# A fused attention and butterfly-FFN kernel: another order for the beginning of its weight fold

## What is computed

```python
x = x + layernorm(x) * scan(0.9, ctx * ctx)          # scan over the 512 tokens of a sequence
h = layernorm(x) @ W_exp + b_exp                     # 512 -> 2048
h = butterfly(h, up_weights)                         # 11 stages of 2x2 pairs, stride 1, 2, ... 1024
h = gelu(h + up_bias)
h = butterfly(h, down_weights)                       # 11 stages again
x = x + h @ W_con + b_con + down_bias                # 2048 -> 512
```

## Time and profile before

| | us |
|---|---|
| median of 3 executions | 2791.27 |
| lowest, highest | 2789.72, 2792.17 |
| span of the profiled execution | 2791.6 |
| TensorE busy in that span | 2739.0 (98%) |
| VectorE busy | 2129.0 (76%) |
| ScalarE busy | 1134.3 (41%) |
| GpSimd busy | 409.5 (15%) |

### The profile page before, as it was taken

One profiled execution on the slowest core, in us unless ns is written; L12 is line 12 of the kernel. 1 busy time (PEld: TensorE's weight loads), 2 busy tenths in 40 slices (PEclk: granted clock), 3 DMA queues, 4 the chain that ended last, 5 costly groups with the idle time before them and its releaser, 6 DMA issues.

```text
span 2791.6 us, 34984 instructions
## 1 busy us (share of the span) xinstructions
PE 2739.0 (98%) x12141; PEld 2255.2 (81%) x12141; DVE 2129.0 (76%) x3562; ACT 1134.3 (41%) x1697; POOL 409.5 (15%) x578
## 2 busy tenths in 40 slices
PE   8779999999999999999999999999999999999998
PEld 5658888888888888888888888888888888888887
DVE  8958777787877778787777878777887877788533
ACT  4843433434343343434334343433434343343432
POOL 5731111020111102011110201111010111102000
PEclk8989999999999999999999999999999999999999
DMA  9795675847557584765758576575847657585543
GB/s 273 250 299 176 175 223 160 239 152 220 185 173 225 160 241 151 219 188 172 225 162 240 152 216 190 169 226 161 241 152 217 190 167 228 156 244 156 181 151 99
DMA packets 294997, 544.67 MB, mean 195 GB/s; under 512 B 37462, under 2 KB 101110, under 8 KB 277670
## 3 DMA queue, kind: packets, MB, share of 16 engines
q1 hardware_dynamic: 287920, 538.91, 63.5%
q0 software_dynamic: 1488, 2.27, 0.4%
q10 hardware_dynamic: 5414, 1.25, 0.3%
HBM read 447.92 MB, written 60.82 MB: 182 GB/s over the span
## 4 chain that ended last, share of the span: by engine, by line
PE 93%; DVE 1%; DMA 1%; issue 0%; ACT 0%; SPq 0%; POOL 0%; DVEq 0%; ACTq 0%
PE ps L1650 43%; PE ps L1668 25%; PE ps L1681 25%; DMA kv<-in_ctx_dram 1%; DMA w_split<-xop 0%; PE ps L1730 0%; DVE w1r L1121 0%; DVE xop L1121 0%; DVE x L1178 0%; POOL raw L479 0%; SPq L537 0%; DVE raw L1175 0%; DMA raw<-kv 0%; DVE kv L1205 0%; DVE raw L1225 0%
## 5 line engine op out<-in xcount | busy, mean ns | idle before, releaser
L1650 PE MATMUL ps<-xop,w1r 128*128 128x512 f32 x5376 | 1366.8, 390 | 7.1 <-ACT st L946 4.6
L1650 PEld LDWEIGHTS ps<-xop,w1r 128*128 128x128 f32 x5376 | 1011.3, 188 | 218.5 <-issue 6.3
L1681 PE MATMUL ps<-w2r,ghi 128*128 128x512 f32 x2032 | 626.6, 390 | 8.2 <-DVE x L1317 8.2
L1668 PE MATMUL ps<-w2r,ghi 128*128 128x512 f32 x2048 | 630.4, 389 | 0.0
L946 ACT ACTIVATE st<-ps 128x512 f32<-128x512 f32 x384 | 229.8, 598 | 839.0 <-PE ps L1650 839.0
L1317 DVE TENSOR_TENSOR x<-ps,x 128x512 f32<-128x512 f32 x508 | 348.9, 687 | 281.1 <-PE ps L1681 278.6
L1681 PEld LDWEIGHTS ps<-w2r,ghi 128*128 128x128 f32 x2032 | 381.8, 188 | 87.8 <-DVE x L1317 8.6
L1668 PEld LDWEIGHTS ps<-w2r,ghi 128*128 128x128 f32 x2048 | 384.4, 188 | 79.8
L1335 DVE TENSOR_TENSOR g<-ps,st 128x512 f32<-128x512 f32 x384 | 262.9, 685 | 217.3 <-PE ps L1650 217.3
L950 ACT ACTIVATE g<-g,gelu_bias 128x512 f32<-128x512 f32 x384 | 275.1, 716 | 369.4 <-DVE g L1335 369.4
L1340 DVE TENSOR_TENSOR glo<-g,ghi 128x512 fp32r<-128x512 f32 x510 | 345.5, 698 | 79.3 <-ACT ghi L964 79.2
(11 more groups left out here) (160 smaller groups left out, 1619.3 us busy)
## 6 DMA issues: line engine op xcount, KB each, us to landing
w1r<-w_products SPq DMA_DIRECT2D x889, 256.0 KB, 3.3
w2r<-w_split SPq DMA_DIRECT2D x128, 1024.0 KB, 5.0
x<-in_x_dram SPq DMA_DIRECT2D x128, 256.0 KB, 7.1
raw<-kv SPq DMA_DIRECT2D x496, 64.0 KB, 2.2
out_dram<-x SPq DMA_DIRECT2D x120, 256.0 KB, 4.0
kv<-in_ctx_dram SPq DMA_DIRECT2D x64, 256.0 KB, 7.4
raw<-in_ctx_dram SPq DMA_DIRECT2D x64, 256.0 KB, 5.2
w_split<-w2s SPq DMA_DIRECT2D x12, 512.0 KB, 7.3
```

What stands on the lines that cost most here:

```text
L1650: last = nc.tensor.matmul(bank[:, :], w1r[:, slot, w, c * P:(c + 1) * P], xop[:, XPOS[m], v, c, :], start=(opens and i == 0), stop=(i == l ...
L1668: last = nc.tensor.matmul(ps_ya[j][:, :], g[:, p % 2, q, j * P:(j + 1) * P], w2r[:, p % 2, kk, w, :], start=(p == 0 and kk == 0 and i == 0 ...
L1681: last = nc.tensor.matmul(ps_yb[:, :], g[:, p % 2, q, j * P:(j + 1) * P], w2r[:, p % 2, kk, w, :], start=(kk == 0 and i == 0), stop=(kk == ...
```

## The change

Seven pieces, all in the order of the lists; no arithmetic is added or taken away.

1. The up side's top stage is spread bank by bank. Bank places become 4, 0, 1, 2 (`TOP_PLACE[0]`); each waits only until the low product that last read its bank is done (`TOP_FREED`), counts `top_spread` for itself, and `top_products` waits per bank. The pieces stand between the last WT steps: two banks ahead of WT 12, one ahead of WT 14, one behind WT 15.
2. VectorE does `top_products(0)` directly behind `low_products(0)`, and `lane_rows(1)` and both `coefs_lo(1)` after it.
3. ScalarE's `square(0, 0)` moves from ahead of WT 12's copy to behind low_up 1's.
4. VectorE does `high_products(0)` ahead of the first `stats1` (it was behind it). GpSimd's list is unchanged: `rstd_rows(0)`, which waits for that `stats1`, stands ahead of `high_matrix(0)`.
5. The down side's `PARTED` spreads leave their place ahead of the high fold and stand inside it, behind high_up 3. `spread_count` and `SPREAD_ORDER` renumber the waits, so the load of `W_con` waits for all twenty spreads.
6. The down side's top spreads (now four counts) move from behind high_up 9 to behind high_up 15; the bias transpose goes one step later, and the 16 bias matmuls come ahead of high_up 15 where they stood behind it.
7. ScalarE's `square(0, 1)` and `neg_ident` move from behind high_up 3's copy to behind high_up 9's.

```diff
@@ -342,6 +342,11 @@
 
         def spreads(dn, stage):
             return dn * (LOWS + HIGH) + stage + 1
+
+        SPREAD_ORDER = (list(range(LOWS + HIGH)), [*range(PARTED[0]), *range(LOWS, LOWS + HIGH), *PARTED])
+
+        def spread_count(dn, stage):
+            return dn * (LOWS + HIGH) + SPREAD_ORDER[dn].index(stage) + 1
         UP_DONE = LOWS + HIGH
         ALL_DONE = 2 * UP_DONE
 
@@ -358,7 +363,9 @@
             return top_src[dn][0:4].rearrange("q (x b) -> q b x", b=2)
 
 
-        TOP_PLACE = (0, 1, 2, 3)
+        TOP_PLACE = ((4, 0, 1, 2), (0, 1, 2, 3))
+        TOPS = len(TOP_PLACE[0])
+        TOP_FREED = (None, PARTED[0] - 1, PARTED[0], LOWS - 1)
 
 
         def w1_columns(w, r):
@@ -513,7 +520,7 @@
             load_tokens(raw[:, 1, :, :], 0, ctx_rows, 1, ctx_loaded[1])
 
             wcon_src = w_con.rearrange("(k e r) d -> (k e) (r d)", e=E, r=R)
-            sp.wait_ge(coef_spread, spreads(1, LOWS - 1))
+            sp.wait_ge(coef_spread, spread_count(1, LOWS - 1))
             for part in range(2):
                 cols = slice(part * R * D // 2, (part + 1) * R * D // 2)
                 sp.dma_start(flat(wcon[:, :, :])[:, cols], wcon_src[:, cols]).then_inc(wcon_loaded[part], NX)
@@ -834,7 +841,7 @@
                     act.wait_ge(bias_low, 1)
                     wait_kept(act, "high_up", R - 1)
                 if n == 1:
-                    act.wait_ge(top_spread, 2)
+                    act.wait_ge(top_spread, 2 * TOPS)
                 for g in groups:
                     if g == 2:
                         act.wait_ge(wsum_ready, 4 * n + 4)
@@ -873,21 +880,21 @@
                     act.dma_start(bias_tmp, down_bias.partition_broadcast(P)).then_inc(bias_loaded, NX)
                     for stage in PARTED:
                         coefs_hi(1, stage)
-                if k == 3 * KH // 4:
-                    square(0, 0)
                 fold_step("WT", k)
             for k in range(KH):
                 fold_step("low_up", k)
+                if k == 1:
+                    square(0, 0)
             top_hi(1)
             act.dma_start(hc_up, up_w[LOW:LOW + HIGH].rearrange("s (m p) a b -> p s m (a b)", p=P))\
                .then_inc(coef_loaded, NX)
             for r in range(R):
                 fold_step("high_up", r)
-                if r == 3:
+                if r == 9:
                     square(0, 1)
                     act.wait_ge(coef_spread, ALL_DONE)
                     act.activation(neg_ident[:, :], ident[:, :], ACT.Copy, scale=-1.0).then_inc(neg_ident_ready, 1)
-                if r == 12:
+                if r == 13:
                     act.wait_ge(bcol_turned, 1)
                     act.activation(bcol, ps[4][:, 256:256 + 2 * KH], ACT.Copy).then_inc(bcol_kept, 1)
             weights_hi(0, (0, 1))
@@ -1046,7 +1053,7 @@
                     cur = (full if (stages - 1 - stage) % 2 == 0 else spare)[:, 0:n]
                     bank, col = places[stage]
 
-                    dve.wait_ge(coef_spread, spreads(dn, first + max(stage, 3)))
+                    dve.wait_ge(coef_spread, spread_count(dn, first + max(stage, PARTED[0] - 1)))
                     if prev is None:
                         last = nc.vector.tensor_copy(cur.rearrange("p (o a l) -> p o a l", o=outer, a=2),
                                                      spread_view(ps[bank][:, col:col + n], first, stage, outer))
@@ -1091,8 +1098,8 @@
 
             def top_products(dn):
                 dve.wait_ge(path_product, spreads(dn, LOWS - 1))
-                dve.wait_ge(top_spread, dn + 1)
-                for c, bank in enumerate(TOP_PLACE):
+                for c, bank in enumerate(TOP_PLACE[dn]):
+                    dve.wait_ge(top_spread, dn * TOPS + c + 1)
                     last = path_stage(nc.vector, flat(LX[:, dn, 4 * c:4 * c + 4, :]), half[:, 2 * c * P:2 * (c + 1) * P],
                                       spread_view(ps[bank][:, :], 0, LOW - 1, KH // 4), LOW - 1)
                 last.then_inc(low_matrix_ready, 1)
@@ -1238,16 +1245,15 @@
                 nc.vector.tensor_copy(top_sel[lane:lane + Q], top_choice[0:Q]).then_inc(top_sel_ready, 1)
             top_lo(0)
             low_products(0)
+            top_products(0)
             lane_rows(1)
-            coefs_lo(1, PARTED[0:1])
-            top_products(0)
-            coefs_lo(1, PARTED[1:2])
+            coefs_lo(1)
             dve.wait_ge(const_ready, 2)
             dve.wait_ge(bias_row_ready, 1)
             for j in range(J):
                 scan_chunk(0, 0, j)
+            high_products(0)
             stats1(0, 0, xs[0], range(J))
-            high_products(0)
             dve.wait_ge(mean1_ready, J)
             stats1(0, 1, xs[0], range(J), means=False)
             for j in range(J):
@@ -1492,16 +1498,19 @@
                                                     start=(bit == 0), stop=(bit == 1))
                     last.then_inc(coef_spread, 1)
 
-                def top():
+                def top(cs):
                     pe.wait_ge(top_sel_ready, 4)
                     pe.wait_ge(coef_lo, dn * PARTS + PARTS)
-                    pe.wait_ge(path_product, spreads(dn, LOWS - 1))
-                    for c, bank in enumerate(TOP_PLACE):
+                    for c in cs:
+                        if dn:
+                            pe.wait_ge(path_product, spreads(dn, LOWS - 1))
+                        elif TOP_FREED[c] is not None:
+                            pe.wait_ge(path_product, spreads(dn, TOP_FREED[c]))
                         for bit in range(2):
-                            last = nc.tensor.matmul(ps[bank][:, :], top_sel[:, c, bit, :],
+                            last = nc.tensor.matmul(ps[TOP_PLACE[dn][c]][:, :], top_sel[:, c, bit, :],
                                                     top_parts[dn][:, bit * 512:(bit + 1) * 512],
                                                     start=(bit == 0), stop=(bit == 1))
-                    last.then_inc(top_spread, 1)
+                        last.then_inc(top_spread, 1)
 
                 def low(stages):
                     pe.wait_ge(low_loaded[dn], LOW_LOADS * NX)
@@ -1575,31 +1584,37 @@
                 if k % 4 == 0:
                     pe.wait_ge(wexp_loaded[k // 4], NX)
                 if k == 3 * KH // 4:
-                    spread_top()
+                    spread_top((0, 1))
+                if k == 3 * KH // 4 + 2:
+                    spread_top((2,))
                 fold_step("WT", k)
+            spread_top((3,))
             pe.wait_ge(low_matrix_ready, 1)
             for k in range(KH):
                 wait_kept(pe, "WT", k)
                 fold_step("low_up", k)
             spread_high(range(HIGH))
-            spread_low_dn(range(LOWS))
+            spread_low_dn(range(PARTED[0]))
             spread_high_dn(range(HIGH))
             pe.wait_ge(high_matrix_ready, 1)
             for r in range(R):
                 if r % 4 == 0:
                     pe.wait_ge(z_loaded[r // 4], NX)
                 fold_step("high_up", r)
-                if r == 9:
-                    spread_top_dn()
-                if r == 11:
+                if r == 3:
+                    spread_low_dn(PARTED)
+                if r == 12:
                     pe.wait_ge(path_product, ALL_DONE)
                     pe.wait_ge(bias_loaded, 4 * NX)
                     nc.tensor.transpose(ps[4][:, 256:256 + 2 * KH], bias_rows, ident[0:2 * KH, 0:2 * KH])\
                         .then_inc(bcol_turned, 1)
-            pe.wait_ge(bcol_kept, 1)
-            for k in range(KH):
-                last = nc.tensor.matmul(ps[4][:, 256 + k:257 + k], LX[:, 0, k, :], bcol[:, k:k + 1], start=True, stop=True)
-            last.then_inc(bias_low, 1)
+                if r == 14:
+                    pe.wait_ge(bcol_kept, 1)
+                    for k in range(KH):
+                        last = nc.tensor.matmul(ps[4][:, 256 + k:257 + k], LX[:, 0, k, :], bcol[:, k:k + 1],
+                                                start=True, stop=True)
+                    last.then_inc(bias_low, 1)
+            spread_top_dn((0, 1, 2, 3))
             pe.wait_ge(high_matrix_ready, 2)
             for q in range(R // 4):
                 fold_step("turn_high", q)
```

## The result

| | before | after |
| --- | --- | --- |
| median, 20 runs each | 2791.07 us | 2795.05 us |
| lowest to highest | 2789.18 to 2792.95 | 2793.54 to 2796.99 |
| profiled execution: span | 2791.6 us | 2795.2 us |

The ratio is 1.0016, with a 95% interval of 1.0009 to 1.0022: the changed kernel is slower by 4.0 us, with an interval of +2.5 to +6.1. The forecast was +3.4 us, 2794.7. The total is right, but two of the steps to it are not, and their errors cancel in the main: that it came so close is luck. The profile after shows both. (Its profiled execution took 2796.99 us, the span and 1.8 around it. By the same 1.8 the profiled execution of before took 2793.4, so both lie some 2 us above their medians.

The account below looks back on a forecast made before the run. VectorE's list was taken to bound the fold. The terms had VectorE leave top_products(1) at 84.65 instead of 81.21, +3.4 us passed one for one to the end: 2794.7 us, range 2793 to 2797.

Parts of the forecast that it names:

- this end does not rest on the hold in piece 4: End of high fold: even with VectorE in time (78.5), TensorE's top spreads still end its wait at 82.2.
- no hold: First gate beside GpSimd's high_matrix(0): lower end, gate takes 0.72 and ends at 55.2, VectorE 0.3 us early.
- all of it: First gate beside high_matrix(0): upper end, gate held until 57.9 instead of 55.53, VectorE 2.4 us late.
- rival 1: End of high fold at half clock: VectorE leaves at 88.5 to 90, kernel +7 to +9 us; chance 0.2.
- my argument against the rival: Half clock: a 2.63 us stop before low_up was followed by steps of 0.87, too fast for half clock.
- I give its shift to the end one for one: After VectorE leaves top_products(1): its whole delay, 3.4 us, reaches the kernel's end.
- No slack to give a delay back, and none to gain: Behind VectorE's top_products(1): between 84 and 129 us VectorE waited only once, 0.5 us.

Follow-up runs that it names:

- a_gp: The changed kernel with GpSimd's high_matrix(0) ahead of rstd_rows(0): 2795.32 us, ratio 1.0015.
- a_bias: The changed kernel with the 16 bias matmuls behind the down side's top spreads: 2790.57 us, ratio 1.0002.
- a_top: The changed kernel with the down side's top spreads behind high_up 11, bias matmuls still ahead of high_up 15: 2791.02 us, ratio 0.9999.
- a_dense: The changed kernel with 17 matmuls of 128 columns in the bias matmuls' place and the bias matmuls last: 2792.91 us, ratio 1.0002.
- d10: The kernel before with ten extra VectorE operations (6.1 us) directly behind top_products(1): 2795.81 us, ratio 1.0019.
- d5: The kernel before with five extra VectorE operations (3.0 us) directly behind top_products(1): 2792.89 us, ratio 1.0008.
- b_up: The kernel before with pieces 1 to 3 of the change alone: 2792.45 us, ratio 1.0003.
- a_bias_gp: a_bias with GpSimd's high_matrix(0) also ahead of rstd_rows(0): 2788.36 us, ratio 0.9990 to the kernel before.

## Why the prediction was right and where it was not

**Pieces 1 to 3**: forecast low_up at 29.4 and the scans at 33.85; measured 28.96 and 33.51. Right, and so is the reason (the row of the scans names ScalarE's square). **Piece 4**: forecast `high_matrix(0)` at 53.6 and the first gate held until 57.9; measured 53.27 and 57.54. Right; a_gp shows the cause, since the hold goes when the two are apart. (One reading on the way was not: at 57.18 GpSimd was not still. It had an operation of 0.60 us beside that gate, from 57.34 on, of a kind that took 0.19 at 64.45. There the gate, which was first, kept its 0.72 and GpSimd's was held.) The choice between no hold and all of it was the upper end, and that is what came. **Piece 5**: parted spreads forecast at 62.75 for 1.5 us, `W_con` issued at 64.4; the timelines of TensorE and SyncE after have

```profile
62.91 1.64 PE L1496 MATMUL ps<-csrc_b,sel_parts 128*128 128x512 f32 x6
64.58 0.82 SPq L526 DMA_DIRECT2D wcon<-in_L_ffn_W_con_dram  x2
...
88.03 2.13 PE L1572 MATMUL ps<-HX,wcon 128*128 128x128 f32 x17
```

and high_dn, which needs `W_con`, started without a wait. It cost nothing, as said.

**Pieces 6 and 7**: the mechanism is the forecast's: VectorE waits for the top spreads, which wait behind the bias matmuls, whatever the gate did ("this end does not rest on the hold in piece 4"). a_bias, a_top and a_gp show each part of that. The size was off. The bias matmuls, priced at 3.63 by the row of before, took 4.86; high_up 15 took 2.06, not 0.85; the top spreads 3.37, not 2.07. That is 3.7 us more, less 0.6 because the bias matmuls started at 76.53 instead of 77.1, and less 0.5 by which the rows overlap: the top spreads ended at 86.33 instead of 83.65, and VectorE left at 87.11 instead of 84.65. This is the mechanism of rival 1, which had a chance of 0.2, though it came later than the 75 us that it was priced for: VectorE left at 87.11 and not at 88.5 to 90. I weighed it by the stops of TensorE; the rows show the clock falling inside the one-column matmuls, and a_dense shows that it stayed up with others in that place, in the one execution profiled. The row on which my argument against the rival rested, the fast low_up behind a stop of 2.63 us, was itself of one execution. The Trainium skill's rule (TensorE: Matmul & The Clock Gate, What's actually happening) that recent activity releases the clock would have favoured this rival. But in the stretch in which the clock fell here TensorE is shown busy for 3.00 of 3.00 us, and in the one ahead of it for 2.41, as in a_dense, so that from its busy time a reader would not have seen the difference.

**"I give its shift to the end one for one"** is the step that did not hold against the kernel before. Rival 1 priced a departure at 88.5 to 90 at +7 to +9; this one at 87.11 became +4.0. By the first profile 6.0 us late became 3.35 at the restart, by the second 4.7 became 3.7; d10 gave 4.6 for 6.1. No interval excludes one for one, but all the values lie below it. It is not that a share of every delay disappears, as the kernels side by side show (us; the fourth column is the median less that of before in the same series, and the second and third are each of one profile):

| | VectorE leaves | first scan on `raw` to last `normalise` | median |
|---|---|---|---|
| before, two profiles | 81.14, 82.41 | 46.5, 46.9 | |
| d5 | 82.93 (scans begin) | 45.7 | +1.7 |
| d10 | 86.93 (scans begin) | 45.0 | +4.6 |
| b_up | 79.30 | 50.7 | +1.4 |
| a_bias_gp | 80.69 | 45.5 | -2.9 |
| a_top | 81.78 | 45.8 | -0.2 |
| a_bias | 82.24 | 45.5 | -0.7 |
| a_dense | 84.33 | 45.5 | +1.6 |
| a_gp | 86.63 | 45.5 | +4.0 |
| changed | 87.11 | 45.5 | +4.0 |

The last six are the changed kernel and the edits to it above. Among them 6.4 us of VectorE's time go with 6.9 us in the medians: there one for one fits. What is missing is missing against before, where VectorE leaves within a microsecond or so of a_bias, a_top and a_bias_gp and needs 0.7 to 1.4 us longer for the same operations. In before TensorE starts turn_high 5.9 and 4.0 us after VectorE has left, in b_up 9.0 after, in the last six at most 3.1 after. That suggests that in before VectorE was already a little early for the other engines, and that a first part of its delay, 1 to 2 us, only took this up. No run moves that alone, so it is not shown. Nor does a profile pair settle it: at the issue of the context's load the shift was still +5.75 by the first and +4.2 by the second, and the rest of the difference is the length of that load in one execution.

**"No slack to give a delay back, and none to gain"** is wrong in its second half as well: b_up gained 0.7 to 3.1 us for VectorE and nothing for the kernel, since ScalarE and TensorE then came last. The wait table of before tells that VectorE did not wait. It does not tell how nearly it would have; in the second profile of before it did, for the same engine:

```profile
DVE w1r L1121 <- ACT w1r L843: 0.4, 1, 0.4
```

**The profile as a starting point**: the forecast took 2791.6 and 2791.27 for the time before. They fit together less well than they look, since a span of 2791.6 belongs to an execution of 2793.4, 2.3 us above the median. The profiled execution after was also a late one, by 1.9, and so the span of 2795.2 met the forecast of 2795.0 so closely; the median missed its own by 0.35.

## What to carry to other kernels

Two losses on one engine do not add where the second is a wait for another engine's fixed time: work out both arrival times, take the later one, and expect an edit to the earlier loss to do nothing until the later one is gone (a_gp +0.3 us, a_bias_gp -2.2 us). Keep what another engine waits for ahead of small slow matmuls that nobody waits for; here the order of two blocks was worth 4.5 us, all that the change lost, and about half of it was the clock. And before a single profile's shift of a microsecond or two is explained, profile the same kernel twice: one early clock fall moved this one by 1.3 us.

## What the hardware showed that I had not expected

- TensorE's granted clock fell while it was shown busy all the time, inside 32 one-column passes (0.65 in the stretch from 78, 0.50 in the next), and it stayed at 1.00 in the same place with 34 passes of 128 columns. It does not fall there every time: of 14 profiles it fell inside such passes in nine, within 0.6 us of their end in three, and not at all in two.
- A stop of 2.6 us on TensorE was followed by a clock of 1.00 in one execution and of 0.69 and 0.74 in another of the same kernel; one of 2.0 to 2.1 us by 0.51 in the first and by 1.00 in the second.
- GpSimd's 3.7 to 4.0 us operation held one VectorE operation with two inputs in SBUF until it was through (3.32 against 0.72) and a `TENSOR_SCALAR` as well (2.92 against 0.54), though not the multiplications that read PSUM (2.44 in both cases). The Trainium skill (SBUF — State Buffer, Who interferes with whom) says that a VectorE instruction with two inputs in SBUF contends with a GpSimd instruction that reads SBUF, that one in a two-port mode contends too, which it says `tensor_scalar` can enter, and that one with at most one input in SBUF outside these modes does not. The traces agree for the first and the last; that the held `TENSOR_SCALAR` ran in such a mode no run shows.
